# Second-order features of a recommendation tower: level 0 in six steps of 128 rows and a half step

## The reference

```python
x0 = e                                                       # [B, 39, 16]
z0 = einsum('bid,bjd->bdij', x0, x0).reshape(B, D, 39 * 39)
cur0 = relu(einsum('bdk,kl->bld', z0, W0))                   # W0: [39 * 39, 128]
next_h, direct0 = split(cur0, 2, axis=1)                     # 64 and 64 rows
z1 = einsum('bid,bjd->bdij', x0, next_h).reshape(B, D, 39 * 64)
cur1 = relu(einsum('bdk,kl->bld', z1, W1))                   # W1: [39 * 64, 128]
z = concatenate([direct0, cur1], axis=1).sum(axis=-1)        # sum over d
y = relu(relu(concatenate([z, dense_ctx], 1) @ W_top1 + b_top1) @ W_top2 + b_top2) @ W_top3
```

## Time and profile before

| | |
|---|---|
| median of 3 runs | 1618.85 us (1618.25 to 1619.11) |
| the profiled execution | 1618.66 us |
| its span, first to last instruction | 1616.9 us |
| TensorE matmuls (PE) | busy 1501.2 us, 93% |
| TensorE weight loads (PEld) | busy 824.7 us, 51% |
| VectorE (DVE) | busy 1447.7 us, 90% |
| ScalarE (ACT) | busy 482.6 us, 30% |
| GpSimd (POOL) | busy 974.7 us, 60% |
| mean granted TensorE clock | 0.994 of full speed |
| DMA | 273.75 MB, 169 GB/s over the span |

### The profile page before, as it was taken

One profiled execution on the slowest core, in us unless ns is written; L12 is line 12 of the kernel. 1 busy time (PEld: TensorE's weight loads), 2 busy tenths in 40 slices (PEclk: granted clock), 3 DMA queues, 4 the chain that ended last, 5 costly groups with the idle time before them and its releaser, 6 DMA issues.

```text
span 1616.9 us, 13509 instructions
## 1 busy us (share of the span) xinstructions
PE 1501.2 (93%) x4496; PEld 824.7 (51%) x4496; DVE 1447.7 (90%) x1315; ACT 482.6 (30%) x495; POOL 974.7 (60%) x628
## 2 busy tenths in 40 slices
PE   0278999999999999999999999999999999999999
PEld 0144555555555555555555555555555555555533
DVE  0267999999999999999999999999999999999920
ACT  0123323333333323232333233232333232322222
POOL 6788888888585858678585858678585830000000
PEclk9989999999999999999999999999999999999999
DMA  3567766767667766677767776677667675663500
GB/s 82 139 157 196 200 187 178 190 178 190 182 189 179 206 187 175 184 179 196 187 175 190 195 196 169 185 187 192 184 177 193 184 206 173 179 184 105 137 1 0
DMA packets 93980, 273.75 MB, mean 169 GB/s; under 512 B 18635, under 2 KB 28747, under 8 KB 93717
## 3 DMA queue, kind: packets, MB, share of 16 engines
q1 hardware_dynamic: 64822, 236.15, 54.5%
q10 hardware_dynamic: 9120, 31.59, 5.7%
q0 software_dynamic: 19968, 5.15, 2.9%
HBM read 241.22 MB, written 31.60 MB: 169 GB/s over the span
## 4 chain that ended last, share of the span: by engine, by line
PE 63%; DVE 23%; issue 10%; POOL 2%; DMA 2%; ACT 0%; DVEq 0%; SPq 0%; ACTq 0%
PE psB L297 31%; PE psA L297 9%; DVE z L510 8%; DVE z_split L510 7%; PE psB L313 5%; DVE z_lo L518 4%; PE psB L306 4%; PE psB L309 4%; DVE r L554 3%; POOL emb L277 2%; PE psB L377 2%; PE psA L289 2%; PE psA L313 2%; PE psA L306 2%; PE psA L309 2%
## 5 line engine op out<-in xcount | busy, mean ns | idle before, releaser
L277 POOL DMA_INDIRECT emb<-in_tbl,ids_all x624 | 974.5, 1562 | 336.0 <-issue 186.5
L297 PE MATMUL psB<-z,w 128*128 128x512 f32 x1664 | 748.1, 593 | 10.1 <-DVE z L510 10.0
L437 ACT ACTIVATE z_hi<-z_split 128x1024 fp32r<-128x1024 f32 (+1 forms) x320 | 338.5, 1058 | 1015.3 <-DVE z_split L510 1003.1
L510 DVE TENSOR_TENSOR z<-h_lay,x_lay 128x1024 f32<-128x1024 f32 x416 | 499.0, 1218 | 11.9 <-DMA h_lay<-h_rows 11.4
L297 PEld LDWEIGHTS psB<-z,w 128*128 128x128 f32 x1664 | 313.3, 190 | 344.3 <-issue 301.4
L518 DVE TENSOR_TENSOR z_lo<-z_split,z_hi 128x1024 fp32r<-128x1024 f32 (+1 forms) x320 | 392.0, 1225 | 1.1 <-ACT z_hi L437 1.1
L510 DVE TENSOR_TENSOR z_split<-h_lay,x_lay 128x1024 f32<-128x1024 f32 x224 | 266.8, 1214 | 0.9 <-DMA h_lay<-h_rows 0.9
L297 PE MATMUL psA<-z,w 117*128 117x512 f32 x512 | 241.8, 595 | 0.0
L306 PE MATMUL psB<-z_hi,w_hi 128*128 128x512 f32 x448 | 183.2, 490 | 0.8 <-ACT z_hi L437 0.5
L313 PE MATMUL psB<-z_lo,w_hi 128*128 128x512 f32 x448 | 145.6, 406 | 21.3 <-DVE z_lo L518 19.4
L297 PEld LDWEIGHTS psA<-z,w 117*128 117x128 f32 x512 | 97.5, 190 | 110.7 <-issue 100.5
(11 more groups left out here) (39 smaller groups left out, 590.8 us busy)
## 6 DMA issues: line engine op xcount, KB each, us to landing
x_lay<-x_rows SPq DMA_DIRECT2D x160, 512.0 KB, 7.0
h_lay<-h_rows SPq DMA_DIRECT2D x128, 512.0 KB, 7.5
x_more<-x_rows SPq DMA_DIRECT2D x96, 512.0 KB, 7.3
x_rows<-x_ring ACTq DMA_DIRECT2D x32, 468.0 KB
base_a<-x_rows SPq DMA_DIRECT2D x32, 468.0 KB
base_b<-x_rows SPq DMA_DIRECT2D x32, 468.0 KB
emb<-in_tbl,ids_all POOLq DMA_INDIRECT x624
h_rows<-r ACTq DMA_DIRECT2D x32, 256.0 KB, 4.4
```

The lines of the kernel that those rows point to most:

```text
L277: nc.gpsimd.indirect_dma_start(emb[t % 2][:, f * D:(f + 1) * D], None, tables[f], bass.IndirectOffsetOnAxis(ids_all[:, t, f:f + 1], 0)).th ...
L297: mm = nc.tensor.matmul(ps[:, cs], w, z[WHOLE_NO[place] % NZ][0:k, cs], start=first, stop=last)
L437: nc.scalar.activation(z_hi[n % NS][0:k, :], z_split[n % NS][0:k, :], ACT.Copy).then_inc(z_hi_made, 1)
L510: nc.vector.tensor_tensor(out[0:k, :], a[0:k, :], b[0:k, :], ALU.mult).then_inc(z_made, 1)
```

## The change

Level 0 gets six steps of all 128 rows and one *half step*. The 780 pairs are laid out anew: 6 x 128 + 64 = 832 rows hold them. The half step has 64 pairs, and its tile of 128 rows x 512 columns holds them twice: rows 0 to 63 for the first 512 columns of the unit, rows 64 to 127 for the last 512. TensorE multiplies rows 0 to 63 into the first bank and rows 64 to 127 into the second (`half_product`). Two new pairs of tiles, `half_a` and `half_b`, are loaded for it in ten DMAs a unit (`load_halves`), which stand in SyncE's list where the third `x_more` stood; that one goes. Each base gets a second DMA for its last 11 rows. `x_ring` and its turn have 128 rows, and the stored ring 178 (128 and 50). The third split step of level 0 is step 5 and no longer step 6, since the last step is now the half step. The weights are packed to match on the host.

```diff
 SH = 3
 ROWS0 = SH * F
-PRODUCTS0 = ((0, 0), (1, 0), (0, 1), (1, 1), (0, 2), (1, 2), (0, 3))
-STEPS0 = len(PRODUCTS0)
-TURNED = 20
-RING = SH * TURNED + ROWS0
+PRODUCTS0 = ((0, 0), (1, 0), (0, 1), (1, 1), (0, 2), (1, 2))
+STEPS0 = len(PRODUCTS0) + 1
+TURNED = (0, 17)
+EXTRA = (63, 72)
+HALF_A = ((11, 49), (29, 15))
+HALF_B = ((29, 10), (1, 39), (8, 15))
+HROWS = P // 2
+WRAP = 6
+RING = SH * 59 + 1
 Q, V = 8, 5
 G, U = 16, 4
 STEPS1 = U * V
 STEPS = STEPS0 + STEPS1
-SPLIT0 = (0, 3, 6)
+SPLIT0 = (0, 3, 5)
 SPLIT1 = (1, 3, 6, 10, 11, 16, 17)
 WHOLE0 = tuple(s for s in range(STEPS0) if s not in SPLIT0)
 WHOLE1 = tuple(s for s in range(STEPS1) if s not in SPLIT1)
 AFTER = (0, 1, 2, 3, 4, 5, 6)
+ORDER0 = SPLIT0 + WHOLE0
...
-        emb = [sb(f"emb{n}", [P, (F + SH - 1) * D]) for n in range(2)]
-        emb_spread = [sb(f"emb_spread{n}", [P, DH, ROWS0]) for n in range(2)]
+        emb = [sb(f"emb{n}", [P, (F + WRAP) * D]) for n in range(2)]
+        emb_spread = [sb(f"emb_spread{n}", [P, DH, SH * (P // SH + 1)]) for n in range(2)]
+        half_a = [sb(f"half_a{n}", [P, BANK]) for n in range(2)]
+        half_b = [sb(f"half_b{n}", [P, BANK]) for n in range(2)]
...
-        w0 = sb("w0", [ROWS0, STEPS0, L])
-        w0_hi = sb("w0_hi", [ROWS0, len(SPLIT0), L], FR)
-        w0_lo = sb("w0_lo", [ROWS0, len(SPLIT0), L], FR)
+        w0 = sb("w0", [P, STEPS0, L])
+        w0_hi = sb("w0_hi", [P, len(SPLIT0), L], FR)
+        w0_lo = sb("w0_lo", [P, len(SPLIT0), L], FR)
...
         def more(u, t):
-            n = (3 * u + t - 1) % NR
+            n = (2 * u + t - 1) % NR
             return x_more[:, n * C:(n + 1) * C]
...
@@ -184,18 +194,28 @@
                 sp.wait_ge(x_stored[u % 2], 32 * (u // 2) + 32)
                 if u >= 2:
                     sp.wait_ge(z_made, at0(u - 2, STEPS0 - 1) + 1)
-                a = x_rows[u, 0:ROWS0:SH, :].unsqueeze(1).to_broadcast([F, SH, C])
-                sp.dma_start(half(base_a, u)[0:ROWS0, :], a).then_inc(base_a_loaded[u % 2], 16)
-                b = x_rows[u, SH * TURNED:RING:SH, :].unsqueeze(1).to_broadcast([F, SH, C])
-                sp.dma_start(half(base_b, u)[0:ROWS0, :], b).then_inc(base_b_loaded[u % 2], 16)
+                for c, (dst, loaded) in enumerate(((base_a, base_a_loaded), (base_b, base_b_loaded))):
+                    first = SH * TURNED[c]
+                    src = x_rows[u, first:first + ROWS0:SH, :].unsqueeze(1).to_broadcast([F, SH, C])
+                    sp.dma_start(half(dst, u)[0:ROWS0, :], src).then_inc(loaded[u % 2], 16)
+                    sp.dma_start(half(dst, u)[ROWS0:P, :], x_rows[u, EXTRA[c]:EXTRA[c] + P - ROWS0, :]).then_inc(loaded[u % 2], 16)
 
             def load_more(u, t):
-                n = 3 * u + t - 1
+                n = 2 * u + t - 1
                 if n >= NR:
-                    pu, pt = divmod(n - NR, 3)
-                    last = max(s for s in range(STEPS0) if PRODUCTS0[s][1] == pt + 1)
-                    sp.wait_ge(z_made, at0(pu, last) + 1)
+                    sp.wait_ge(z_made, at0(u - 2, 2 * t + 1) + 1)
                 sp.dma_start(more(u, t), x_rows[u, 3 * SH * t:3 * SH * t + P, :]).then_inc(more_loaded[n % NR], 16)
+
+            def load_halves(u):
+                if u >= 2:
+                    sp.wait_ge(z_made, at0(u - 2, STEPS0 - 1) + 1)
+                for dst, loaded, runs in ((half_a, half_a_loaded, HALF_A), (half_b, half_b_loaded, HALF_B)):
+                    for n in range(2):
+                        p = HROWS * n
+                        for f, rows in runs:
+                            src = x_rows[u, SH * f:SH * (f + rows - 1) + 1:SH, n * BANK:(n + 1) * BANK]
+                            sp.dma_start(dst[u % 2][p:p + rows, :], src).then_inc(loaded[u % 2], 16)
+                            p += rows
 
             def load_lay(u, v):
                 n = V * u + v
@@ -227,15 +247,16 @@
                 if u + 1 < UNITS:
                     load_lay(u + 1, 1)
                 if 0 < u < UNITS - 2:
-                    load_more(u + 2, 3)
+                    load_halves(u + 2)
                 if u + 1 < UNITS:
                     for k in range(U):
                         load_hlay(u + 1, k)
                     load_lay(u + 1, 2)
                 if u == 0:
                     load_bases(2)
-                    for t in range(1, 4):
+                    for t in range(1, 3):
                         load_more(2, t)
+                    load_halves(2)
 
...
             load_bases(0)
-            for t in range(1, 4):
+            for t in range(1, 3):
                 load_more(0, t)
+            load_halves(0)
             load_lay(0, 0)
             load_bases(1)
-            for t in range(1, 4):
+            for t in range(1, 3):
                 load_more(1, t)
+            load_halves(1)
...
                 for d in range(DH):
-                    last = nc.tensor.transpose(half(psA, u)[0:ROWS0, d * P:(d + 1) * P], emb_spread[u % 2][:, d, :], ident[:, :])
+                    last = nc.tensor.transpose(half(psA, u)[:, d * P:(d + 1) * P], emb_spread[u % 2][:, d, 0:P], ident[:, :])
                 last.then_inc(x_turned, 1)
 
             def product(ps, place, k, w, first, last):
@@ -295,6 +318,15 @@
                 for c in range(C // BANK):
                     cs = slice(c * BANK, (c + 1) * BANK)
                     mm = nc.tensor.matmul(ps[:, cs], w, z[WHOLE_NO[place] % NZ][0:k, cs], start=first, stop=last)
+                mm.then_inc(z_used, 1)
+
+            def half_product(ps, place, w):
+
+                pe.wait_ge(z_made, place + 1)
+                for n in range(2):
+                    rows = slice(n * HROWS, (n + 1) * HROWS)
+                    mm = nc.tensor.matmul(ps[:, n * BANK:(n + 1) * BANK], w[rows, :],
+                                          z[WHOLE_NO[place] % NZ][rows, 0:BANK], start=False, stop=True)
                 mm.then_inc(z_used, 1)
             def step0(u, s):
                 if s == 0:
                     pe.wait_ge(x_kept, u + 1)
-                if s in SPLIT0:
+                if s == STEPS0 - 1:
+                    half_product(half(psA, u), at0(u, s), w0[:, ORDER0.index(s), :])
+                elif s in SPLIT0:
                     n = SPLIT0.index(s)
-                    split_product(half(psA, u), at0(u, s), ROWS0, w0_hi[:, n, :], w0_lo[:, n, :], s == 0, s == STEPS0 - 1)
+                    split_product(half(psA, u), at0(u, s), P, w0_hi[:, n, :], w0_lo[:, n, :], s == 0, False)
                 else:
-                    product(half(psA, u), at0(u, s), ROWS0, w0[:, s, :], s == 0, s == STEPS0 - 1)
+                    product(half(psA, u), at0(u, s), P, w0[:, ORDER0.index(s), :], s == 0, False)
...
             def wrap(t):
                 act.wait_ge(gathered[t % 2], 16 * F * (t // 2) + 16 * F)
-                nc.scalar.activation(emb[t % 2][:, F * D:], emb[t % 2][:, 0:(SH - 1) * D], ACT.Copy).then_inc(wrapped, 1)
+                nc.scalar.activation(emb[t % 2][:, F * D:], emb[t % 2][:, 0:WRAP * D], ACT.Copy).then_inc(wrapped, 1)
...
                 e = emb[u // 2 % 2][:, :]
-                src = bass.AP(e.tensor, e.offset + DH * (u % 2), [list(e.ap[0]), [1, DH], [D, F], [D, SH]])
-                dst = emb_spread[u % 2][:, :, :].rearrange("p d (f b) -> p d f b", f=F)
+                src = bass.AP(e.tensor, e.offset + DH * (u % 2), [list(e.ap[0]), [1, DH], [D, P // SH + 1], [D, SH]])
+                dst = emb_spread[u % 2][:, :, :].rearrange("p d (f b) -> p d f b", b=SH)
                 nc.scalar.activation(dst, src, ACT.Copy).then_inc(spread, 1)
 
             def keep_x(u):
@@ -408,10 +442,10 @@
                 if u >= 2:
                     act.wait_ge(x_stored[u % 2], 32 * (u // 2))
                     act.wait_ge(z_made, at0(u - 2, 1) + 1)
-                nc.scalar.activation(half(x_ring, u)[0:ROWS0, :], half(psA, u)[0:ROWS0, :], ACT.Copy).then_inc(x_kept, 1)
+                nc.scalar.activation(half(x_ring, u), half(psA, u), ACT.Copy).then_inc(x_kept, 1)
                 act.wait_ge(x_kept, u + 1)
-                act.dma_start(x_rows[u, 0:ROWS0, :], half(x_ring, u)[0:ROWS0, :]).then_inc(x_stored[u % 2], 16)
-                act.dma_start(x_rows[u, ROWS0:RING, :], half(x_ring, u)[0:RING - ROWS0, :]).then_inc(x_stored[u % 2], 16)
+                act.dma_start(x_rows[u, 0:P, :], half(x_ring, u)).then_inc(x_stored[u % 2], 16)
+                act.dma_start(x_rows[u, P:RING, :], half(x_ring, u)[P - ROWS0:RING - ROWS0, :]).then_inc(x_stored[u % 2], 16)
...
                     if s in SPLIT1:
                         high(at1(u, s), P)
                     if s in AFTER and AFTER.index(s) in SPLIT0 and u + 1 < UNITS:
-                        high(at0(u + 1, AFTER.index(s)), ROWS0)
+                        high(at0(u + 1, AFTER.index(s)), P)
...
-            nc.scalar.activation(w0_hi[:, :, :], w0[:, 0:STEPS0:3, :], ACT.Copy).then_inc(w0_hi_made, 1)
```

(87 more changed lines are left out.)

2 lines of the change are left out of this document (1 added, 1 removed).

## The result

The changed kernel takes **1682.53 us** (median of 4 runs, 1678.83 to 1683.33) against 1618.98 us for the kernel before in the same series: the ratio is 1.0381, with a 95% interval of 1.0369 to 1.0394. The forecast was 1635.5 us with a range of 1626 to 1665. The direction was right, the size was not: 63.5 us lost instead of 16.6, beyond the top of the range.

What follows compares the result with a forecast made beforehand. VectorE was taken to set the pace between about 156 and 1542 us. 1618.66 - 16.1 (half product) + 31.0 (rounding wait) + 1.8 (start) = 1635.4, forecast as 1635.5 us, range 1626 to 1665.

Steps and rivals of the forecast that it cites:

- The half product: VectorE's level 0: one product of 512 columns instead of 1024 saves 0.52 us in 31 units, 16.1 us gained.
- The stalled rounding: `keep_x` between two ScalarE roundings makes VectorE's subtraction wait 1.07 us in 29 units, 31.0 us lost.
- TensorE: Half step taken as 1.72 us; TensorE's unit of 43.1 to 45.4 us stays hidden behind VectorE's 45.85.
- Rival D: Half step on TensorE costs more than 3.6 us and passes VectorE's pace; 1654 us at 4.2 us; chance 3%.
- SyncE and the DMAs: Later bases and ten small issues, 0.5 us each and ended by 822, stay hidden ahead of the `h_lay` loads.
- The cover itself: First `h_lay` load lands 4.4 us after issue, 3.05 us before VectorE's product needs it, plus 0.5 from the longer unit.
- Rival B: Ten small DMAs and late bases push `h_lay` loads beyond their cover: 15 to 45 us, 1650 to 1680; chance 20%.
- The start: Two early waits for bases grow with each base's second DMA, by 0.8 and 1.0 us: 1.8 us lost.

Runs made afterwards that it cites:

- the run at full width: Changed kernel with `keep_x` one step earlier, and VectorE making all 1024 columns of the half step's product: 1698.27 us, +1.0 us on the kernel before.
- `keep_x` early: Changed kernel with `keep_x` one step earlier in ScalarE's list, ahead of the roundings of step 5: 1680.14 us against 1697.30 for the kernel before.

## Why the prediction was right and wrong

- **The half product**: right. 16.1 us forecast; pitch 45.28 to 44.74, 0.54 x 31 = 16.7 us, and 18.2 us by the run at full width.
- **The stalled rounding**: right in place and size. 29 x 1.07 = 31.0 forecast, 30.3 us in the list (1.1 before), 0.99 in the unit shown. `keep_x` held ScalarE for 1.88 us up to the next rounding; I had 1.8.
- **TensorE**: hidden, as said; 1.06 us and not the 1.72 that I took, and VectorE waits for TensorE in no row of the list. Rival D had no ground.
- **SyncE and the DMAs**: here the prediction failed. The sentence that failed is that the ten issues are "ended by 822: hidden", together with the place of the `h_lay` loads "today at 822.24 behind the store of h". The issues were right (4.3 us). But I kept the landing of the store as it is in today's kernel (817.97 to 822.24, and 4.4 us in the median). It is a transfer on the same DMA engines as the batch whose shift by 7 us I had just worked out. My own numbers spoke against it: 2.6 MB issued some 9 us ahead of it take 10 us at my 250 GB/s. It took 7.7 us, 3.3 more, which is the whole of the 3.05 us of cover. I had put the backlog behind the cover, as something that eats part of it, and not ahead of the store that the cover begins with.
- **The cover itself** was read too wide, and this makes the rest of the 1.5 us a unit (44.7 us in 30 units). I took 4.4 us for the landing of the first `h_lay` load, the least in the earlier trace rows. Its median in the kernel before is 4.6 us between 500 and 1300 us, which leaves 2.8 us of cover. In the unit shown above the store adds 3.4 us and the load takes 5.2: 3.4 + 0.6 - 2.8 = 1.2, and 1.14 were waited. The second load I did not look at. Issued at 822.85, with a median of 6.5 us, and needed at 831.96, it has 2.6 us of cover; in the kernel after it takes 7.3, and 0.29 us more were waited for it. The product that needs it, kernel before:

```profile
831.96 1.21 DVE L510 TENSOR_TENSOR z_split<-h_lay,x_lay 128x1024 f32<-128x1024 f32 x1
```

- **Rival B** had the right symptom and price (15 to 45 us; 44.7 measured), for the wrong cause (slow issues, uneven engines), and so only 20%. The sum with it is 1635.5 + 44.7 = 1680.2, and the range stopped at 1665. What the Trainium skill, DMA: Bandwidth & Descriptors, "Why a DMA increments its semaphore by 16 and not by 1", says on the number of engines, and what I held for this rival, decided nothing: the ten DMAs do no harm with `keep_x` early (-17.2 us), and the harm is there without them (+65.8 us).
- **The start**: 1.8 us forecast. The wait for the first base grew by 1.9 (57.3 to 59.2) and that for the first `h_lay` by 3.8 (11.4 to 15.2).
- **The sum** of what the lists show, in the profiled runs: -16.7 + 29.2 + 43.8 + 5.7 = 62.0 us, against 64.6 of span. The 2.6 us left over are not assigned.

## What to carry to other kernels

Moving one item in an engine's list moves all the DMAs behind it: work out what is then in flight when the next critical transfer starts, and give that transfer the time it takes in that company, not the one it takes today. An instruction with slack of several microseconds in a list can be moved freely only up to the next pair that runs hand over hand with the bounding engine; here one step's place was worth 73 us (+56.2 against -17.2, each against the kernel before on its own chip). When a change frees time on an engine that doesn't bound, look for a trade that moves work there: the half step alone gave 17 us, with one split step made whole it gave 35. And look at what a shortened instruction was covering: the half product no longer covers a rounding.

## What the runs showed of the hardware

- A store of 256 KB on ScalarE's queue lands in 4.4 us or in 7.6 us (medians of the two pages), with 1.0 or 1.5 MB of SyncE's queue still to be moved when it is issued. The Trainium skill, DMA: Bandwidth & Descriptors, "Queues, rings and completion order", says that each DMA engine takes turns between the queues that it has work for. The traces agree: between the first and the last packet of the store 0.5 MB of SyncE's queue move in the changed kernel and 1.1 MB in the one with the bases behind the second `x_lay`, and none in the kernel before (medians). But in the changed kernel the first packet also starts later, 4.1 us after the issue against 3.1; why, no run shows.
- Two float32 matmuls of 64 rows, in different halves of the rows and for different banks, run side by side: 1.06 against 1.91 us for the step. The Trainium skill, TensorEngine Tiling (Array Packing), "Tiling Modes", says that row tiles run independently, and the run agrees. The drain that it adds for a change of mode is not seen by itself; by these rows it is at most some 0.2 us a step, what lies above the bare pitch (an estimate).
- The wait for the first `h_lay` differs between chips: 15.2 us for the changed kernel on the first, 78.2 on another, and 66.7 to 79.2 in all runs on the three other chips. The cause stays open.
